# First attention of a two-layer kernel: another order of three score banks, the block maximum one unit later, and a VectorE loop of 8 steps

## The reference

```python
q = _split_heads(x @ Wq.T + bq)
k = _split_heads(x @ Wk.T + bk)
v = _split_heads(x @ Wv.T + bv)
scores = jnp.einsum('hbnd,hbmd->hbnm', k, q) * SCALE
attn = jax.nn.softmax(scores, axis=-1)
out = jnp.einsum('hbnm,hbmd->hbnd', attn, v)
```

## Time and profile before

| | |
|---|---|
| median of 3 runs | 4616.59 us |
| the profiled execution | 4627.79 us, its span 4626.2 us |
| the attention's steps | about 206 to 2723 us of the span |
| TensorE busy (matmul) over the span | 94% |
| VectorE, ScalarE busy over the span | 77%, 66% |
| granted TensorE clock, mean | 0.963 of full speed |

### The profile page before, as it was taken

The page is one execution under the profiler, slowest core; times in us unless marked ns, Lnnn a source line. Parts: engine busy times, 40 slices in busy tenths (PEclk is TensorE's granted clock), DMA queues, the critical chain, the costliest instruction groups (busy, mean ns, idle before and its releaser), DMA issues. The chain is left out here.

```text
span 4626.2 us, 107866 instructions
## 1 busy us (share of the span) xinstructions
PE 4349.7 (94%) x36307; PEld 2687.5 (58%) x36307; DVE 3562.9 (77%) x4059; ACT 3065.5 (66%) x5554; POOL 911.9 (20%) x1768
## 2 busy tenths in 40 slices
PE   6599999999999999999999969999986699999999
PEld 5244444444444444444444438888866578888887
DVE  5699999999999999999999976566444565555554
ACT  2188888788887888888888855444464354444444
POOL 5212211111212112111111110000002122222222
PEclk8699999999999999999999989999987799999999
DMA  5400100100101001003121130010010422222222
GB/s 192 92 16 13 30 14 13 28 13 14 30 13 31 13 13 30 13 14 67 42 48 32 42 106 28 19 37 27 5 41 28 152 78 84 87 87 87 87 87 88
DMA packets 237632, 225.08 MB, mean 49 GB/s; under 512 B 129024, under 2 KB 197552, under 8 KB 236096
## 3 DMA queue, kind: packets, MB, share of 16 engines
q1 hardware_dynamic: 195840, 142.47, 12.4%
q0 software_dynamic: 41344, 76.61, 5.3%
HBM read 174.67 MB, written 60.36 MB: 51 GB/s over the span
## 5 line engine op out<-in xcount | busy, mean ns | idle before, releaser
L824 DVE TENSOR_REDUCE PM<-A 128x2 f32<-128x1024 f32 x2092 | 2456.5, 1221 | 117.6 <-PE A L713 85.2
L801 ACT ACTIVATE PR<-SB 128x512 f32<-128x512 f32 x4100 | 2121.3, 602 | 366.6 <-PE SB L726 355.7
L746 PE MATMUL PV<-PR,VH 128*32 128x256 f32 x16384 | 1293.6, 387 | 4.3 <-issue 4.3
L713 PE MATMUL A<-QST,KA 48*128 48x512 f32 x4184 | 1194.4, 476 | 59.3 <-DMA QF<-QFD 33.7
L746 PEld LDWEIGHTS PV<-PR,VH 128*32 128x32 f32 x16384 | 432.4, 110 | 557.0 <-issue 369.3
L713 PEld LDWEIGHTS A<-QST,KA 48*128 48x128 f32 x4184 | 428.3, 187 | 518.9 <-issue 413.8
L726 PE MATMUL SB<-KST,QST 50*128 50x512 f32 x3075 | 688.2, 411 | 0.1
L726 PEld LDWEIGHTS SB<-KST,QST 50*128 50x128 f32 x3075 | 387.5, 187 | 205.9 <-ACT PR L801 202.7
L734 PE MATMUL SB<-KF,QF 99*32 99x512 bf16 x4100 | 414.7, 385 | 5.2 <-issue 3.3
L2043 DVE TENSOR_TENSOR m_h_lo<-m_h,m_h_hi 128x512 fp32r<-128x512 f32 x320 | 221.4, 692 | 250.9 <-ACT m_h_hi L1951 250.9
L1951 ACT CAST m_h_hi<-m_h 128x512 fp32r<-128x512 f32 x320 | 187.9, 587 | 257.9 <-DVE m_h L2040 255.9
(11 more groups left out here) (278 smaller groups left out, 5703.1 us busy)
## 6 DMA issues: line engine op xcount, KB each, us to landing
m_shares<-CW POOLq DMA_DIRECT2D x512, 128.0 KB, 2.8
QST<-QS SPq DMA_DIRECT2D x54, 256.0 KB, 9.0
KST<-KS SPq DMA_DIRECT2D x402, 32.0 KB, 1.8
QS<-parts SPq DMA_DIRECT2D x16, 512.0 KB, 5.0
KS<-parts SPq DMA_DIRECT2D x16, 512.0 KB, 4.9
m_x<-X SPq DMA_DIRECT2D x16, 512.0 KB, 3.9
moe_w_lo<-W SPq DMA_DIRECT2D x16, 512.0 KB, 10.1
KF<-KFD SPq DMA_DIRECT2D x402, 16.0 KB, 1.7
```

The lines of the kernel that those rows point to most:

```text
L713: return nc.tensor.matmul(A[:, u % 2 * 2 + e, :], keys, QST[rows, slot, j * TB:(j + 1) * TB], start=True, stop=True)
L746: mm = nc.tensor.matmul(PV[at:at + 2 * HD, 0:HB], VH[:, slot, e, c, :], PR[:, (2 * c + e) % P_SLOTS, b * HB:(b + 1) * HB], start=(c == 0), ...
L801: nc.scalar.activation(PR[:, v % P_SLOTS, :], SB[:, s_bank(v), :], ACT.Exp, scale=SCALE).then_inc(s_free, 1)
L824: nc.vector.tensor_reduce(PM[:, par, :, i, j:j + 1], A[:, u % 2 * 2:u % 2 * 2 + 2, :], AX.X, ALU.max).then_inc(a_free, 1)
```

## The change

Three edits, all in the first attention.

1. The list of banks for the 64 score units is made by a function. It goes round 0, 1, 2 up to unit 22. Unit 23 takes the bank of unit 21 (not of unit 20), from which on the order is 2, 1, 0. Unit 43 takes the bank of unit 41, and the order is 0, 1, 2 again; it closes at 64. So units 3 and 4 have different banks, and unit 4 waits for the exp of unit 1. Units 23 and 43, both of the kind `unit_fine`, wait for the exp two places back, units 24 and 44 for the one four places back, all others for three.
2. VectorE takes unit 0 of the next block before the reduction to `neg` of this block.
3. VectorE's loop holds 8 steps and runs 8 times (before: 2 steps, 32 times).

```diff
 S_BANKS = 3
+MAX_RUN = 8
...
+def score_banks():
+
+    banks = [1, 2]
+    for v in range(EXPS):
+        banks.append(banks[-2] if v in TURNS_BACK else sum(range(S_BANKS)) - banks[-1] - banks[-2])
+    return banks[2:]
+
+
+TURNS_BACK = (4 * 5 + 3, 4 * 10 + 3)
+SCORE_BANKS = score_banks()
+
+
 def s_bank(v):
 
-    return (v if v < 4 else v + 2) % S_BANKS
+    return SCORE_BANKS[v]
...
                 def block_max(b, par):
-                    for u in range(MC):
+                    for u in range(1, MC):
                         unit_max(b, u, par)
+                    unit_max(b + 1, 0, 1 - par)
                     dve.wait_ge(a_free, count((b + 1) * MC + 2))
...
                 dve.sem_inc(a_free, 2)
-                with dve.Fori(0, STEPS // 2) as two:
-                    for par in range(2):
-                        block_max(two * 2 + par, par)
+                unit_max(0, 0, 0)
+                with dve.Fori(0, STEPS // MAX_RUN) as run:
+                    for n in range(MAX_RUN):
+                        block_max(run * MAX_RUN + n, n % 2)
                 block_max(STEPS, 0)
-                for u in range(LEAD + 2):
+                for u in range(1, LEAD + 2):
                     unit_max(STEPS + 1, u, 1)
```

## The result

| | median | lowest to highest | ratio to before, 95% interval |
|---|---|---|---|
| before | 4617.12 us | 4611.48 to 4623.05 (6 runs) | |
| after | 4647.94 us | 4647.18 to 4654.9 (6 runs) | 1.0069 [1.0056, 1.0082] |

The change makes the kernel 31 us slower (4647.94 - 4617.12). 4651 was forecast, 34.4 us over the median then known.

The account below looks back on a forecast made before the run. TensorE's stream was taken to set the pace, VectorE close behind. -13.8 - 9.9 + 41.6 + 16.5 = +34.4 us, added to the median of 4616.6, gave 4651 us; 4622 to 4668 leaves about 0.2 out.

Parts of the forecast that it names:

- Term 1: Group of score units 4 to 7: unit 4 waits for unit 1's exp, 2.60 us falls to 2.385; -13.8 us.
- Term 2: Block's end on VectorE: branches hidden behind unit 0 of the next block, 31 x 0.32 us saved; -9.9 us.
- Term 3: Units 23 and 43: waiting for the exp two back costs 2 x 64 x 0.325 us; +41.6 us (35 to 48).
- Term 4: VectorE's loop of 523 instructions: 7 returns wait for instructions and lower TensorE's clock, 2.35 us each; +16.5 us.
- rival B: VectorE's loop returns do not fetch, 523 instructions behave like 188; +17.9, so 4634 us (4628 to 4641); chance 0.20.
- C: Added turns at units 23 and 43 are free, only the loop returns' fetch is paid; 4609 us; chance 0.08.
- D: Added turns at unit 23 and its like and VectorE's returns both free; -23.7, so 4593 us; chance 0.06.
- E: Stalls at VectorE's returns or the added turns pull the clock down; above 4668 us; chance 0.06.
- VectorE's 523 is nearest to SyncE's 496: VectorE's loop return: taken as 2.2 us more than today, since SyncE's loop of 496 instructions needs 2.5 us.

Follow-up runs that it names:

- the best version: The kernel before with turns at units 20 and 40, unit 0 ahead of the reduction, VectorE's loop of 2 steps: 4588.69 us, ratio 0.9935.

## Why the prediction was right, step by step

- **Term 1** (unit 4, -13.8 us): 16 us by the turns alone, with 10 to 21 in the interval. Right.
- **Term 2** (the block's end, -9.9): 13 us by the order alone, 9 to 17. Right in size, and its reason as well: the sequencer does the branch behind unit 0. That the reduction comes a unit later cost nothing, as forecast. But the term is no gain of the changed kernel beside the turn at unit 43, since that turn takes the long groups behind the branches away by itself; the prediction did not see that the two stalls overlap. The total doesn't suffer, since it takes those groups off only once.
- **Term 3** (the added turns, +41.6): 36 us, 29 to 44, by the run with turns at the fourth unit against that with turns at the first. The mechanism is the forecast one to the hundredth: the load comes 1.90 us after the group's start, which is 1527.22 in the reckoning from the earlier trace rows. What was too large were the 0.05 us allowed for a bare weight load: the group lasts 2.67, near the lower end of 2.66 to 2.76. 128 x 0.285 = 36.5.
- **Term 4** (the returns, +16.5): 26 us, 19 to 33. The mechanism is right, the term too small. The trace of the changed kernel, where the seven cost 21 us, says by which part. The standstill was put at 1.5 us and cost 2.0 on average: the fetch took 2.8 to 3.0 us and not 2.5, and the next unit came 1.87 us late. The clock was put at 0.85 us each and cost 1.0, but not in the way assumed: not a part of the loss at each return, but 1.4 to 3.0 us at three of them and nothing at four.

The kernel with edits 1 and 2 and a short loop is terms 1 to 3 alone. Its forecast, the same as rival B's, is +17.9 us (11 to 24); it was 6 us slower (2 to 10). So terms 1 to 3 together were 12 us too high: 5 or 6 of them are term 3, and the rest lies in terms 1 and 2, which were forecast at 24 us where the best version is 30 us faster (24 to 36). The groups counted in the traces don't explain this rest, and it stays open. Term 4 was 9 us too low. The two errors cancel, and that the total of +34.4 is within 4 us of the measured 31 is luck. The sign is not: the banks with the order, and the long returns, each cost time by themselves (6 and 26 us), and each term was measured by itself.

Rival B is out by the 2.8 us of each return, C and D by the waits at line 747. What E names is there, a lower clock behind three of the seven returns, but far too small for its 4668.

The step "VectorE's 523 is nearest to SyncE's 496" held. The counts of 496 and 188 given ahead of the prediction leave out instructions that only wait for or raise a semaphore: with these SyncE's loop has 512 and the feed-forward loop 224, while VectorE's loop in the attention has none of them. From the rule in the Trainium skill, "Runtime: NRT & Kernel Launch", section Instruction fetch mechanics, I had concluded for the loop of 6 steps that what fits into 512 instructions is not fetched. That is not so here; it was my reading of the rule as one of length.

## What to carry to other kernels

A rotation of buffers that doesn't close should be turned where the needed release comes early enough. Compare the end of the release with the time at which the load goes anyway, place by place: the same turn costs between 0 and 0.9 us here. A longer loop body to save branches can cost more than it saves: here 31 short branches cost some 13 us, an instruction moved in front of them made them free, and seven long returns cost some 26. And before you add up the gains of two edits, ask whether the stalls that they remove fall together.

## What the runs showed of the hardware

- A return in VectorE's loop took 0.2 to 0.3 us with a body of 133 or 263 instructions, and 2.7 to 3.1 us with 393 or 523. Straight code of 64 steps had no such wait. The Trainium skill, "Runtime: NRT & Kernel Launch", section Instruction fetch mechanics, says that a taken branch waits for a fetch if its target is outside the current window of two pages of code, and that code is loaded in blocks of 256 instructions. The waits and the packets of the instruction queue agree with such a fetch. The run with 393 shows that a loop of fewer than 512 can wait too; whether the place of its start in a page decides was not tried.
- An idle time of TensorE of 1.53 to 1.82 us was followed by a lower granted clock at some returns and not at others: at three of seven in the changed kernel (0.50 to 0.66 over the next 5 us) and at five of nine in the loop of 6 (0.66). Its length doesn't decide within this range: the clock fell behind 1.54 and 1.55 us, and stayed at 1.00 behind 1.70, 1.74 and 1.81. No run here settles what decides.
- The waits list put VectorE's 1.79 us at a return down to TensorE. The register operations of the sequencer, not the list, showed the cause.
